# A stencil and masked-attention kernel on one core: last tile off TensorE's stencil, pair 10 on it, and a reordered start and tail

## The reference

```
lap_x = (left - 2x + right)        # along the 512 columns, reflected at the edges
lap_y = (above - 2x + below)       # along the 2048 rows, reflected at the edges
x1  = x + zX*lap_x + zY*lap_y + zR*x*(1-x)
s   = tanh(x1 @ W1 + b1) @ v       # one score per row
p   = softmax(s masked by type)    # type 0: l<=j, type 1: l>=j, type 2: l!=j
out = x1 + (p @ x1) / count(j)
```

## Time and profile before

| | us |
|---|---|
| runs of the kernel before | 109.46, 109.75, 110.18 |
| median | 109.75 |
| profiled execution, its own time | 110.17 |
| profiled execution, span from first to last instruction | 108.4 |
| TensorE / VectorE / ScalarE / GpSimd busy | 100.6 / 88.6 / 75.5 / 68.2 |

### The profile page before, as it was taken

How to read it: one execution, slowest core, us unless ns; L and a number is a source line. 1 busy time by engine, 2 the same in 40 slices (tenths; PEclk the granted TensorE clock), 3 DMA queues, 4 the chain that set the end, 5 groups by cost and what they waited for, 6 DMA issues and landing times. The chain is left out here.

```text
span 108.4 us, 1739 instructions
## 1 busy us (share of the span) xinstructions
PE 100.6 (93%) x416; PEld 59.6 (55%) x416; DVE 88.6 (82%) x129; ACT 75.5 (70%) x170; POOL 68.2 (63%) x86
## 2 busy tenths in 40 slices
PE   6999999989999998999899989998999999997950
PEld 3344578684675466556555655565565554664320
DVE  4489899589979999999999999999999685146680
ACT  0836576858789598769876986798789662758610
POOL 5799999989998994999599859974500100010000
PEclk9999999999999999999999999999999999999995
DMA  3899999979989999999999999984423253035574
GB/s 90 249 313 341 390 387 388 388 280 317 296 280 345 348 364 379 372 395 388 391 384 395 386 399 394 364 334 138 138 91 100 79 186 119 3 98 169 166 234 148
DMA packets 16741, 29.89 MB, mean 276 GB/s; under 512 B 1811, under 2 KB 2325, under 8 KB 16729
## 3 DMA queue, kind: packets, MB, share of 16 engines
q1 hardware_dynamic: 16668, 29.70, 77.6%
q10 hardware_dynamic: 60, 0.07, 0.2%
HBM read 21.37 MB, written 8.39 MB: 275 GB/s over the span
## 5 line engine op out<-in xcount | busy, mean ns | idle before, releaser
L1008 PE MATMUL hps<-x1T,W1s 128*128 128x512 f32 (+1 forms) x72 | 29.7, 555 | 0.3 <-ACT x1T L383 0.3
L1067 PE MATMUL U<-X,M 128*128 128x512 f32 x60 | 28.9, 602 | 0.6 <-ACT M L426 0.6
L587 POOL TENSOR_TENSOR lr<-xin 128x1020 f32<-128x1020 f32 (+1 forms) x16 | 29.3, 1832 | 0.0
L593 POOL TENSOR_TENSOR sq<-ab 128x1024 f32<-128x1024 f32 x12 | 28.3, 2362 | 1.3 <-DMA ab<-in_x 1.3
L804 DVE SCALAR_TENSOR_TENSOR outs<-U,fac,X 128x512 f32<-128x512 f32 x30 | 21.6, 747 | 9.3 <-ACT X L447 8.4
L374 ACT ACTIVATE xps<-xin,cdia,nzR 128x1024 f32<-128x1024 f32 x11 | 13.3, 1207 | 9.6 <-DVE X L748 9.6
L997 PE MATMUL tps<-ident,X 128*128 128x128 f32 x132 | 17.6, 276 | 2.0 <-DVE X L748 1.9
L997 PEld LDWEIGHTS tps<-ident,X 128*128 128x128 f32 x132 | 15.0, 142 | 7.6 <-issue 4.2
L638 POOL TENSOR_TENSOR cs<-cs,e 128x2 f32<-128x2 f32 x16 | 3.1, 192 | 25.3 <-ACT e L403 24.2
L1008 PEld LDWEIGHTS hps<-x1T,W1s 128*128 128x128 f32 x72 | 13.0, 190 | 10.8 <-issue 10.0
L383 ACT ACTIVATE x1T<-tps 128x512 f32<-128x512 f32 x33 | 17.7, 587 | 1.4 <-PE tps L997 1.3
(11 more groups left out here) (120 smaller groups left out, 86.0 us busy)
## 6 DMA issues: line engine op xcount, KB each, us to landing
ab<-in_x SPq DMA_DIRECT2D x48, 256.0 KB, 5.1
out<-outs SPq DMA_DIRECT2D x32, 252.0 KB
xin<-in_x SPq DMA_DIRECT2D x30, 256.0 KB, 6.0
xin<-in_x SPq DMA_DIRECT2D x2, 252.0 KB
W1s<-in_L_cond_W SPq DMA_DIRECT2D x1, 256.0 KB, 5.9
xin<-in_x SPq DMA_DIRECT2D x2, 66.0 KB
xin<-in_x SPq DMA_DIRECT2D x6, 2.0 KB
out<-outs SPq DMA_DIRECT2D x1, 64.0 KB
```

Source lines behind the costliest of these rows:

```text
L587: pool.tensor_tensor(to[:, :, 1:D - 1], src[:, :, 0:D - 2], src[:, :, 2:D], ALU.add).then_inc(s_lr, 1)
L593: pool.tensor_tensor(sq[:, p % 3, :, :], near[:, m % 2, 0, :, :], near[:, m % 2, 1, :, :], ALU.add).then_inc(s_ud, 1)
L1008: last = mm(hps[:, part], W1s[:, c, :], x1T[:, k % 2, c, part], start=(c == 0), stop=(c == DC - 1))
L1067: mm(bank(j), weights, X1[:, i, :], start=True, stop=True).then_inc(s_U, 1)
```

## The change

- Pair 16 (the last tile) moves into `ASIDE`, pair 10 out of it. So the last tile has shifted loads (six small DMAs), an addition on GpSimd, a factor on ScalarE and three VectorE instructions of 512 columns, where it had one matmul, a square and two VectorE instructions. Pair 10 has two matmuls of 512 columns, a square of 1024 columns and two VectorE instructions instead of three.
- The third tridiagonal matrix is no longer made.
- zY and zR are loaded by SyncE ahead of x, zX alone by ScalarE. The warm matmuls go from 512, 512 and 512 columns to 512, 320 and 384.
- The small matmul that spreads the types (`tall`) moves from the opening to round 3.
- The shifted copies get four buffers instead of two.
- ScalarE's order in round 3 is that of the rounds around it, without the factor of pair 10; in the tail, weights(7) now stand between the carries. The last carry, the last sum and the last output are each cut into two halves of columns; the last sum has its own PSUM banks.

```diff
-ASIDE = (3,) + tuple(range(5, 16))
+ASIDE = (3, 5, 6, 7, 8, 9) + tuple(range(11, 17))
...
             def load_near(p):
                 m = aside(p)
-                if m > 2:
-                    sp.wait_ge(s_ud, m - 2)
+                if m > NS:
+                    sp.wait_ge(s_ud, m - NS)
...
+            sp.dma_start(zrow[:, 1, :], zY.rearrange("(o n) -> o n", o=1)).then_inc(s_small, 16)
+            sp.dma_start(zrow[:, 2, :], zR.rearrange("(o n) -> o n", o=1)).then_inc(s_small, 16)
             load(0)
...
-            for q, zz in enumerate((zX, zY, zR)):
-                act.dma_start(zrow[:, q, :], zz.rearrange("(o n) -> o n", o=1)).then_inc(s_small, 16)
+            act.dma_start(zrow[:, 0, :], zX.rearrange("(o n) -> o n", o=1)).then_inc(s_small, 16)
...
+            def carry_last():
+                at, to = carried(LAST - 1)
+                act.wait_ge(s_U, LAST)
+                act.wait_ge(s_T, to + 1)
+                for cols in HALVES:
+                    nc.scalar.activation(X1[at:at + 1, to, cols], bank(LAST - 1)[0:1, cols], ACT.Copy).then_inc(s_cy, 1)
...
-                if k >= 1 and 2 * k + 4 in ASIDE:
+                if k == 0:
+                    factor_of_x(2 * k + 5)
+                    counted(k)
+                    weights(k)
+                elif k + 1 < KG:
+                    if 2 * k + 4 == PAIRS - 1:
+                        factor_of_x(PAIRS - 1)
                     carry(j + 2)
                     carry(j + 3)
                     counted(k)
-                if 2 * k + 5 in ASIDE:
-                    factor_of_x(2 * k + 5)
-                if k >= 1 and 2 * k + 4 not in ASIDE:
+                    if 2 * k + 5 < PAIRS:
+                        factor_of_x(2 * k + 5)
+                    weights(k)
+                else:
+                    weights(k, (0, 1))
                     carry(j + 2)
+                    weights(k, (2,))
                     carry(j + 3)
-                if k + 1 < KG and (k == 0 or 2 * k + 4 not in ASIDE):
-                    counted(k)
-                weights(k)
+                    weights(k, (3,))
             weights_last()
...
+            def output_last():
+                to = outs[:, LAST % OS, :]
+                dve.wait_ge(s_f, KG + 1)
+                dve.wait_ge(s_store[LAST % OS], 16 * (LAST // OS))
+                for h, cols in enumerate(HALVES):
+                    dve.wait_ge(s_Uy, h + 1)
+                    vec.scalar_tensor_tensor(out=to[:, cols], in0=tps[:, h, 0:D // 2], scalar=fac[:, LAST:TILES], in1=X1[:, LAST, cols],
+                                             op0=ALU.mult, op1=ALU.add).then_inc(s_o, 1)
...
-                    dve.wait_ge(s_cz2, 4)
-                    tridiagonal(2)
                     first_carries()
...
+                if k == TYPES:
+                    pe.wait_ge(s_tf, 1)
+                    mm(tall, unit, tfrow[:, :], start=True, stop=True).then_inc(s_ty, 1)
...
+            def pooled_last():
+                pe.wait_ge(s_M, TILES)
+                pe.wait_ge(s_cz, LAST - 1)
+                for h, cols in enumerate(HALVES):
+                    pe.wait_ge(s_cy, h + 1)
+                    mm(tps[:, h, 0:D // 2], Mz[:, :], X1[:, LAST, cols], start=True, stop=True).then_inc(s_Uy, 1)
...
-            warm(512, 512)
+            warm(512, 320)
...
-            warm(512)
+            warm(384)
...
-                if 2 * k + 4 < PAIRS - 1 and 2 * k + 4 not in ASIDE:
+                if k == 0:
+                    stencil(4)
+                scores(k)
+                if k >= 1 and 2 * k + 4 < PAIRS and 2 * k + 4 not in ASIDE:
                     stencil(2 * k + 4)
-                scores(k)
...
-                if 2 * k + 4 == PAIRS - 1:
-                    stencil(PAIRS - 1)
```

More of the change, by code:

```diff
@@ L155, in build @@
         s_A = sem("s_A")
-        s_near = [sem(f"s_near_slot{k}") for k in range(2)]
+        s_near = [sem(f"s_near_slot{k}") for k in range(NS)]
         s_u = sem("s_u")
@@ L259, in near_loaded @@
         def near_loaded(p):
-            return 16 * sum(5 if q < NB else 4 for q in ASIDE if q <= p and (aside(q) - aside(p)) % 2 == 0)
+            return 16 * sum(6 if q == PAIRS - 1 else 4 for q in ASIDE if q <= p and (aside(q) - aside(p)) % NS == 0)
         def stored(q):
@@ L293, in load_near @@
                 m = aside(p)
-                if m > 2:
-                    sp.wait_ge(s_ud, m - 2)
+                if m > NS:
+                    sp.wait_ge(s_ud, m - NS)
+                to, done = near[:, m % NS, :, :, :], s_near[m % NS]
+                if p == PAIRS - 1:
+                    for n in range(NB):
+                        at = HALF * n
+                        sp.dma_start(to[at:at + REST + 1, 0, 0, :], x[n, S - REST - 2:S - 1, :]).then_inc(done, 16)
+                        sp.dma_start(to[at:at + REST, 1, 0, :], x[n, S - REST:S, :]).then_inc(done, 16)
+                        sp.dma_start(to[at + REST:at + REST + 1, 1, 0, :], x[n, S - 2:S - 1, :]).then_inc(done, 16)
+                    return
                 for h, i in enumerate(tiles_of(p)):
@@ L299, in load_near @@
                         at = r - 2 + 2 * q
-                        sp.dma_start(near[:, m % 2, q, h, :], x[n, at:at + P, :]).then_inc(s_near[m % 2], 16)
+                        sp.dma_start(to[:, q, h, :], x[n, at:at + P, :]).then_inc(done, 16)
             def store(j):
@@ L415, in exp_last, with weights @@
                                      bias=bia[:, 1:2], scale=scl[:, 1:2]).then_inc(s_e, 1)
-            def weights(k):
+            def weights(k, which=range(GB)):
                 act.wait_ge(s_e, k + 1)
@@ L423, in weights @@
                     act.wait_ge(s_msk, 2)
-                for m in range(GB):
+                for m in which:
                     i = in_order(GB * k + m)
@@ L509, in _ @@
                     carry(j + 1)
-                if 2 * k + 4 in ASIDE:
+                if 2 * k + 4 in ASIDE and 2 * k + 4 < PAIRS - 1:
                     factor_of_x(2 * k + 4)
@@ L817, in ending @@
                 factors_last()
-                output(LAST)
+                output_last()
             settings()
@@ L1065, in pooled @@
                     pe.wait_ge(s_o, j - 1)
-                weights = Mz[:, :] if j == LAST else M4[:, k % 2, i - GB * k, :]
-                mm(bank(j), weights, X1[:, i, :], start=True, stop=True).then_inc(s_U, 1)
+                mm(bank(j), M4[:, k % 2, i - GB * k, :], X1[:, i, :], start=True, stop=True).then_inc(s_U, 1)
+            def pooled_last():
[4 more added lines that the diff above has]
+                    mm(tps[:, h, 0:D // 2], Mz[:, :], X1[:, LAST, cols], start=True, stop=True).then_inc(s_Uy, 1)
             def warm(*widths):
```

58 lines of the change are left out of this document (34 added, 24 removed).

## The result

| | before | after |
|---|---|---|
| median of 7 runs each | 109.88 us | 110.85 us (110.46 to 111.10) |
| the profiled execution | 110.17 | 111.10 |
| its span | 108.4 | 109.4 |

The ratio after to before is 1.0089, 95% interval 1.0071 to 1.0108: slower by 0.9%, where 0.5 us faster was forecast. The time lies above the forecast's range.

What follows compares the result with a forecast made beforehand. VectorE with ScalarE in its loop bounds the steady rounds, TensorE the start, round 1 and tail. Terms -0.32 -0.30 +1.13 -0.86 -0.26 +0.10 = -0.51, set against median 109.75, gave 109.2 us; range 107.9 to 110.4.

Steps and rivals of the forecast that it cites:

- The opening, -0.62: Opening: earlier first stencil -0.32 and types' matmul moved out -0.30, together -0.62 us.
- it is gained in full: Opening: TensorE waits for nothing from the types' matmul to the scores at 21.75, so removing it gives -0.30 us.
- The -0.32: First stencil: starts 0.65 us earlier, runs that long at half speed if the clock rises at the same moment, gains 0.32.
- Round 2, 0: Round 2: pair 10's square on ScalarE delays kept tiles about 1 us, covered by slack and TensorE's idle time; 0, worst +0.3.
- Round 3, +1.13: Round 3: pair 10's stencil (1.72) and types' matmul (0.30) on TensorE delay pair 12's multiply from 64.39 to 65.52 us.
- The first rival: Rounds 3 and 4: TensorE absorbs the stencil and VectorE stays the bound; -2.89 in all, 106.9 us; chance 0.13.
- the mixture (0 to 0.4): Round 3 costs only 0 to 0.4 through larger ScalarE and VectorE slack; about -1.4 in all, 108.4 us; chance 0.18.
- The tail's matmul, -0.86: Tail: removing pair 16's matmul from TensorE's gapless row at 87.08 saves 0.86 us.
- What is late next is its eviction: Tail: the last tile's eviction ends near 90.9, TensorE needs it at 90.95; a tie counted as hidden, 0 to +0.2.
- The second rival: Tail: the last tile's eviction or the carries hold TensorE by what the removed matmul freed; +0.35, 110.1 us; chance 0.14.
- Weights and halves, -0.26 + 0.10: Tail: weights ahead of the carries let tile 28's sum start 0.26 us earlier; halving last carry, sum and output costs 0.10.
- The clock (third rival): First stencils: shorter warm matmuls leave a gap, TensorE's clock rises later; +1.6, 111.4 us, or 113 with two; chance 0.08.

Runs made afterwards that it cites:

- early sums: Kernel after with GpSimd's sums of rounds 0 and 1 ahead of the shifted copies' addition of pairs 5 and 7: 109.83 to 113.14 us, ratio 1.0261 to before.
- pair 10 aside: Kernel after with pair 10 back on the shifted copies, its stencil off TensorE: 109.26, 112.02, 109.59 and 111.37 us, no ratio formed.
- early decision: VectorE's decision moved to round 0: in after with before's warm-up and types' matmul in round 0, 109.77 us (0.9986 of before); in before, decision alone, 109.81 us (0.9997).

## Why the prediction was wrong

**The opening, -0.62.** Mis-sized, and the step that failed is "it is gained in full". On TensorE the types' matmul and the warm columns were gained, and more (0.86 to 1.37 at pair 4's stencil). But the lengths of round 0 need GpSimd's sums, and GpSimd's queue did not move. The forecast never asked what the lengths wait for once TensorE is early, and the first line of the earlier trace rows shows the product at 24.37 idle for 0.33 us behind ScalarE, so TensorE was not the only one that set the pace there. What reached T0 is 0.41 in the two profiles compared, and nearly nothing against the other two profiles with the opening of before. The early sums gave 0.6 to 1.0. The -0.32 rests on the clock level of one execution: in the other two, both passes of the third warm matmul took 1.13 us together where the earlier trace rows have 2.08.

**Round 2, 0.** Right. With pair 10 on TensorE the product of round 3 comes 0.45 later behind that of round 2 (10.96 against 10.50), and T0 doesn't feel it: it is 27.84 behind the product of round 1 with pair 10 on TensorE and without.

**Round 3, +1.13.** Right in mechanism and size: +1.22, with each of its marks (T0 + 5.35, T0 + 13.38), and undone by pair 10 aside. The first rival, TensorE absorbing the stencil, is out, and so is the mixture (0 to 0.4): the stencil costs 0.71 even without the types' matmul behind it. One mark was not as described: TensorE was not idle ahead of the stencil, its scores had slipped to fill that time.

**The tail's matmul, -0.86.** This step failed, and with it the sign. Exactly 0.86 went from TensorE's row, and none reached the end. "What is late next is its eviction" looked at the tile's own path and found a tie, rightly: the transposes at 91.80 are on time. Late next was VectorE's first output behind its branch. From T0, VectorE's last decision instruction came 1.97 later than before (38.67 to 40.64): round 3's 1.22, and 0.75 for the third instruction of the last tile. 0.73 of that was covered, as output 24 had so much to spare, and the rest, 1.25, is what T0 to S grew (43.90 to 45.15). The profile of before had the gap of 3.61 us in VectorE's timeline, and the prediction has no term and no rival for it: it was taken as nothing, with 0.73 us to spare. The prediction's own mark for this part, the stretch from W to the end 0.2 shorter, came out 1.05 longer (20.10 to 21.15). The second rival came nearest in its effect, the tail's gain lost (110.1), but not by its mechanism; without the jump its place was the tie of the forecast in two kernels (7.84), and in three it cost 0.28, with the unexplained idle time in front of it.

The Trainium skill, in Runtime: NRT & Kernel Launch, section Instruction fetch mechanics, says that branching breaks the sequential prefetch: a taken branch to a target outside the current window of pages stalls until the target has been fetched. The runs agree: the gap shrinks by at least 2.0 us when the arm follows the branch, and with the flag decided long before, load and far jump still take 2.9 to 3.0. That it is the fetch and not another part of the jump no run here shows.

**Weights and halves, -0.26 + 0.10.** Right: -0.11 together (-0.18 up to tile 28's sum, +0.07 behind it), and tile 28's sum is released by the output (0.45), no longer by a weight.

**The clock (third rival)** did not decide the result: after's profiled stencil took 1.98, and its 7 runs lie within 0.7 us. A level that rises late does occur, in two profiles of variants, and its price was well sized (3.7 forecast for four slow passes, 3.78 measured). That the shorter warm matmuls bring it about, as the rival has it, is not shown.

**The set of terms.** With the measured ones: -0.41 + 1.22 - 0.86 + 0.89 - 0.11 + 0.27 = +1.0. The first and the last are within what like kernels differ by; the four between them, +1.14, repeat.

## What to carry to other kernels

When a step is taken off one engine's queue, follow what that engine waits for next on every other engine up to the end, also those that were in time by under a microsecond; a gap that "costs nothing" costs nothing only up to its cover, so write the cover down. Where a long gap that no row explains stands next to a branch, suspect the branch: decide early, load the flag early, keep instructions from piling up ahead of the jump, and test it as here, since the early decision was worth 0.88 us in one kernel and nothing in the other. Cut traces by a few events and compare the stretches: values that repeat to 0.03 us across kernels tell parts apart where whole times scatter by 2 us. And look first which stretches repeat between profiles of the same code; the opening here did not, to 0.4 us.

## What the runs showed of the hardware

- A register load and a jump over the long way on VectorE took 2.88 to 3.02 us where the flag had been written long before (four profiles), and 3.61 to 3.77 where it was written just ahead (six). The jump alone lies between 2.0 and 2.26, each bound from one profile. The page shows them as idle time with another engine's name.
- With a jump over the same code at the end of VectorE's program the span ended 3.34 and 3.51 us behind the last output, against 2.77 to 3.22 in the profiles without it; the kernel before became 0.57 us slower by it.
- The two additions to TensorE's round 3 cost 0.71 (the stencil) and 0 (the types' matmul) alone, and 1.22 together: the slack is used once.
- TensorE's first stencil took 3.78 us instead of 1.98 in two profiles, with the granted clock at 1.00 in the row. The row read 1.00 for the slow warm passes of every opening looked at, so at the start the passes' durations have to be read instead.
